# Audio tower on one core: expert up weights loaded tile by tile into a ring of eight instead of kept and copied on chip

## The reference

```python
# _L0_tok_ref: patches of 16 steps, 90 channels -> 192 features
h = einsum('bnf,ef->bne', patches, W) + b                 # 64 clips x 15 tokens, f = 1440
# _L0_attn_ref on layernorm(h): one head of 192 over the 15 tokens of a clip
qkv = einsum('bnd,de->bne', x, W_qkv) + b_qkv
context = einsum('bqk,bkd->bqd', softmax(q k^T / sqrt(192)), v)
h = h + context
# _L0_ffn_ref on layernorm(h): 16 experts, the best 4 of each token
t = rmsnorm(x, norm_scale)
top_vals, top_idx = top_k(t gate_w^T + gate_b, 4);  route_w = softmax(top_vals)
u = einsum('nh,ech->nec', t, mlp1_w) + mlp1_b             # 192 -> 768, per expert
a = swiglu(u)                                             # limit 7, 768 -> 384
y = einsum('nec,ehc->neh', a, mlp2_w) + mlp2_b            # 384 -> 192
h = h + (x + einsum('neh,ne->nh', y, comb))               # comb: the routing weights
```

## Time and profile before

| what | value |
|---|---|
| median of 3 runs | 297.06 us (295.59 to 300.19) |
| the profiled execution | 297.97 us, span 296.1 us |
| TensorE busy | 261.7 us (88%) |
| VectorE, ScalarE, POOL busy | 168.8, 113.4, 174.2 us |
| mean granted TensorE clock | 0.913 |
| DMA | 32.86 MB, mean 111 GB/s |
| from 34 to 68 us | TensorE busy 34.0 us |
| from 200 to 250 us | TensorE busy 50.0 us, DMA share 0.37 |

### The profile page before, as it was taken

How to read it: one execution, slowest core, us unless ns; L and a number is a source line. 1 busy time by engine, 2 the same in 40 slices (tenths; PEclk the granted TensorE clock), 3 DMA queues, 4 the chain that set the end, 5 groups by cost and what they waited for, 6 DMA issues and landing times.

```text
span 296.1 us, 6296 instructions
## 1 busy us (share of the span) xinstructions
PE 261.7 (88%) x1943; PEld 253.7 (86%) x1943; DVE 168.8 (57%) x427; ACT 113.4 (38%) x291; POOL 174.2 (59%) x202
## 2 busy tenths in 40 slices
PE   2869999998757899999999999999999999999800
PEld 1869999998535699999999999999999999999700
DVE  0020246557788647667666666676677666666500
ACT  1001111224307235555455555455555455555200
POOL 5011146668799614667776767766666876663422
PEclk9995999999755579999999999999999999999955
DMA  6999999999999151334333334333333432443211
GB/s 178 231 193 238 242 225 225 269 249 245 266 269 218 43 133 30 57 44 62 53 56 47 60 51 59 56 48 51 58 57 49 66 58 42 56 60 41 26 19 13
DMA packets 18734, 32.86 MB, mean 111 GB/s; under 512 B 3725, under 2 KB 12269, under 8 KB 18701
## 3 DMA queue, kind: packets, MB, share of 16 engines
q1 hardware_dynamic: 6887, 21.60, 30.5%
q0 software_dynamic: 8640, 9.22, 21.4%
q10 hardware_dynamic: 3174, 1.63, 2.4%
HBM read 26.39 MB, written 6.06 MB: 110 GB/s over the span
## 4 chain that ended last, share of the span: by engine, by line
PE 28%; DMA 28%; issue 16%; POOL 11%; POOLq 7%; DVE 5%; SPq 2%; ACT 0%; DVEq 0%
DMA out<-hn_all,put_row 23%; PE bank L908 8%; POOL hn_all L460 7%; POOLq L467 6%; PE bank L1102 5%; DMA qkvw<-in_qkv_w 5%; POOL out L476 4%; PE bank L945 2%; PE bank L937 2%; PE bank L917 1%; PE bank L1051 1%; PE bank L1111 1%; PE bank L954 1%; PE bank L985 1%; DVE x_sb L817 1%
## 5 line engine op out<-in xcount | busy, mean ns | idle before, releaser
L1102 PE MATMUL bank<-xT,x_sb 96*128 96x128 f32 (+1 forms) x1080 | 137.0, 277 | 0.8 <-DVE x_sb L861 0.8
L1102 PEld LDWEIGHTS bank<-xT,x_sb 96*128 96x128 f32 (+1 forms) x1080 | 131.8, 193 | 1.2 <-issue 1.2
L476 POOL DMA_INDIRECT out<-hn_all,put_row x45 | 71.4, 1586 | 56.2 <-DMA out<-hn_all,put_row 24.1
L460 POOL DMA_INDIRECT hn_all<-t_rows,get_row x45 | 50.5, 1121 | 14.7 <-issue 13.4
L1111 PE MATMUL bank<-w_sb,tokw 128*128 x270 | 51.5, 327 | 0.7 <-DVE tokw L883 0.7
L908 PE MATMUL bank<-tokw,x_sb 120*120 120x192 f32 x192 | 38.7, 365 | 6.7 <-DMA x_sb<-in_x 6.7
L1111 PEld LDWEIGHTS bank<-w_sb,tokw 128*128 128x128 f32 x270 | 42.9, 190 | 1.0 <-issue 1.0
L908 PEld LDWEIGHTS bank<-tokw,x_sb 120*120 120x120 f32 x192 | 36.2, 209 | 7.7 <-DMA x_sb<-in_x 7.7
L872 DVE TENSOR_SCALAR ln_all<-bank 128x384 f32<-128x384 f32 x45 | 25.1, 558 | 28.7 <-PE bank L1102 28.7
L876 DVE TENSOR_TENSOR ln_all<-ln_all 128x384 f32<-128x384 f32 x45 | 25.2, 559 | 26.5 <-ACT ln_all L628 26.5
L607 ACT COPY x_sb<-w_sb 96x768 f32 x45 | 37.1, 824 | 6.5 <-PEq L1094 4.2
(11 more groups left out here) (144 smaller groups left out, 237.4 us busy)
## 6 DMA issues: line engine op xcount, KB each, us to landing
w_sb<-in_w SPq DMA_DIRECT2D x16, 576.0 KB, 17.7
x_sb<-in_x SPq DMA_DIRECT2D x7, 675.0 KB, 10.0
w_sb<-in_w SPq DMA_DIRECT2D x16, 288.0 KB, 19.9
t_rows<-hn_all ACTq DMA_DIRECT2D x8, 90.0 KB, 8.5
hn_all<-t_rows,get_row POOLq DMA_INDIRECT x45, 3.2
out<-h ACTq DMA_DIRECT2D x1, 720.0 KB, 5.1
out<-hn_all,put_row POOLq DMA_INDIRECT x45, 3.5
tokw<-in_tok_w SPq DMA_DIRECT2D x1, 540.0 KB, 7.0
```

The costliest lines, as they stand in the source:

```text
L460: g.indirect_dma_start(out=xg[slot], out_offset=None, in_=t_rows, in_offset=bass.IndirectOffsetOnAxis(ap=get_row[:, m:m + 1], axis=0),).th ...
L476: g.indirect_dma_start(out=out, out_offset=bass.IndirectOffsetOnAxis(ap=put_row[:, m:m + 1], axis=0), in_=ysb[m % RING], in_offset=None, c ...
L1102: ins = t.matmul(dst[:, m * SLOTS:(m + 1) * SLOTS], stage[0:rows, j % 2, c, o:o + 128], xT[0:rows, j % 2, c, :], start=(c == 0), stop=(c = ...
```

## The change

The up weights are no longer kept. `w1_sb` becomes a ring of eight buffers. SP reads the owner of each tile and loads that expert's up weights and their bias for the tile, when the tile of eight before has made its second half. TensorE multiplies straight out of the ring. The copies, `stage`, `here` and their semaphores go. Besides: the attention weights are loaded ahead of x of tile 1, the fold stands between the embeddings of tiles 0 and 1, and POOL's first root stands ahead of its wait for the small loads; SP, not ScalarE, stores h, behind two tiles' weights; the down weights come four per tile; the three later bias products stand ahead of the row sums, and their additions ahead of the copy of the rows; the scatter drops rows past the output, so that the extra rows aren't filled, and padding counts as one owner.

```diff
-SETTLED = 12
+WRING = 8
-        w1_sb = sb("w1_sb", [128, E * W1E])
+        w1_sb = sb("w1_sb", [128, WRING * W1E])
...
+        w1_ring = w1_sb[0:HK + 1, :].rearrange("p (b c n) -> p b c n", b=WRING, c=HC)
...
@@ block.sync
-            def load_expert(e):
-                sp.dma_start(w1_sb[0:HK, e * W1E:(e + 1) * W1E], w1[e]).then_inc(s_w[e], 16)
-                sp.dma_start(w2_sb[:, e * W2E:(e + 1) * W2E], w2[e]).then_inc(s_w[e], 16)
+            def load_down(e):
+                sp.dma_start(w2_sb[:, e * W2E:(e + 1) * W2E], w2[e]).then_inc(s_w2, 16)
+
+            sp.dma_start(tokb_sb[:, :], tok_b.broadcast_to([TT, H])).then_inc(s_tokb, 16)
+            sp.dma_start(qkvw_sb[:, :, 0:3 * H + 1], qkv_w).then_inc(s_qkvw, 16)
+            sp.dma_start(qkb_sb[:, :], qk_b).then_inc(s_qkvw, 16)
+            sp.dma_start(vb_sb[:, :], v_b.broadcast_to([TT, H])).then_inc(s_small, 16)
             for i in range(1, TILES):
...
+                if i > RING:
+                    for e in range(4 * (i - RING - 1), 4 * (i - RING)):
+                        load_down(e)
+            sp.wait_ge(s_owner, 1)
+            experts = []
+            for j in range(MT):
+                if j % GROUP == 0:
+                    experts.extend(owners(mybir.EngineType.SP, j // GROUP))
+                if j == 2:
+                    sp.wait_ge(s_b2c, 4)
+                    sp.dma_start(out[0:TOKENS, :].rearrange("(i p) n -> p i n", p=TT), h[:, :, :]).then_inc(s_base_out, 16)
+                if j >= WRING:
+                    sp.wait_ge(s_lin, j - WRING + 1)
+                b = j % WRING
+                sp.dma_start(w1_sb[0:HK, b * W1E:(b + 1) * W1E],
+                             w1[bass.ds(experts[j], 1)].rearrange("a p n -> (a p) n")).then_inc(s_w1[b], 16)
+                sp.dma_start(w1_sb[HK:HK + 1, b * W1E + 2 * I:(b + 1) * W1E],
+                             b1[:, bass.ds(experts[j], 1), :].rearrange("a e n -> (a e) n")).then_inc(s_w1[b], 16)
...
@@ block.gpsimd
-            pool.wait_ge(s_small, 16 * N_SMALL)
             for i in range(AHEAD):
                 root(i)
+                if i == 0:
+                    pool.wait_ge(s_small, 16 * N_SMALL)
                 v_bias(i)
...
                                      in_=ysb[m % RING], in_offset=None, compute_op=ALU.add,
+                                     bounds_check=TOKENS - 1, oob_is_err=False,
...
@@ block.scalar
-            act.wait_ge(s_w[0], 32)
-            act.dma_start(out[TOKENS:TOKENS + SLOTS, :], w2_sb[:, 0:H]).then_inc(s_base_out, 16)
...
-                a.copy(stage[0:HK, j % 2, 0, :], w1_sb[0:HK, bass.ds(experts[j] * W1E, 2 * I)]).then_inc(s_stage_0, 1)
...
-            act.wait_ge(s_b2c, 4)
-            act.dma_start(out[0:TOKENS, :].rearrange("(i p) n -> p i n", p=TT), h[:, :, :]).then_inc(s_base_out, 16)
...
@@ block.vector
             d.tensor_copy(owned[:, :], ps_owner).then_inc(s_owner, 1)
+            dve.wait_ge(s_base, TILES)
+            for q in range(4):
+                dve.wait_ge(s_b2, q + 1)
+                d.tensor_tensor(h[:, 2 * q:2 * q + 2, :], h[:, 2 * q:2 * q + 2, :], ps_b2[q],
+                                ALU.add).then_inc(s_b2c, 1)
             dve.wait_ge(s_rows, 1)
...
-            for back in (1, 2):
-                d.scalar_tensor_tensor(out=landed[:, back - 1, back:MT], in0=owned[:, back:MT],
-                                       scalar=float(E), in1=landed[:, back - 1, back:MT],
-                                       op0=ALU.is_ge, op1=ALU.max).then_inc(s_apart, 1)
...
-                d.tensor_copy(stage[:, j % 2, 1, :],
-                              w1_sb[0:HK + 1, bass.ds(experts[j] * W1E + 2 * I, 2 * I)]).then_inc(s_stage_1, 1)
...
@@ block.tensor
-            for i in range(AHEAD):
-                embed(i)
-            pe.wait_ge(s_small, 16 * N_SMALL)
-            pe.wait_ge(s_qkvw, 16)
+            embed(0)
+            pe.wait_ge(s_qkvw, 32)
             fold_weights()
             pe.wait_ge(s_const, 7)
             turn_h(0)
+            embed(1)
+            pe.wait_ge(s_small, 16 * N_SMALL)
...
             bias2(0)
-
+            bias2(1)
             pe.wait_ge(s_ended, 1)
             t.matmul(ps_owner, ones[0:E, 0:1], ended[:, :], start=True, stop=True).then_inc(s_own, 1)
+            pe.wait_ge(s_pos, 1)
+            for q in range(2, 4):
+                bias2(q)
...
-                        ins = t.matmul(dst[:, m * SLOTS:(m + 1) * SLOTS], stage[0:rows, j % 2, c, o:o + 128],
+                        ins = t.matmul(dst[:, m * SLOTS:(m + 1) * SLOTS], w1_ring[0:rows, j % WRING, c, o:o + 128],
...
-                pe.wait_ge(s_stage_0, j + 1)
-                pe.wait_ge(s_stage_1, j + 1)
+                pe.wait_ge(s_w1[j % WRING], 32 * (j // WRING + 1))
...
+                    if j == 1:
+                        pe.wait_ge(s_w2, 16 * E)
                     down(j - 1)
```

More of the change, by code:

```diff
@@ L212, in audio_tower_kernel @@
         s_qkvw = sem("s_qkvw")
[L213 to L216, removed]
+        s_w1 = [sem(f"s_w1_{b}") for b in range(WRING)]
+        s_w2 = sem("s_w2")
+        N_SMALL = 5
         s_tokb = sem("s_tokb")
@@ L592, in copy_weight @@
             def copy_weight(j):
+                if j % GROUP == 0:
+                    experts.extend(owners(mybir.EngineType.Activation, j // GROUP))
                 if j >= GATHERS:
@@ L596, in copy_weight @@
                 a.copy(weight[:, slot:slot + 1], xg[slot][:, bass.ds(experts[j] + H, 1)]).then_inc(s_weight, 1)
-            def stage_half(j):
-                if j == 0:
-                    act.wait_ge(s_rows, 1)
-                act.wait_ge(s_here, min(j, SETTLED) + 1)
-                if j >= 2:
-                    act.wait_ge(s_lin, j - 1)
-                if j % GROUP == 0:
-                    experts.extend(owners(mybir.EngineType.Activation, j // GROUP))
-                a.copy(stage[0:HK, j % 2, 0, :], w1_sb[0:HK, bass.ds(experts[j] * W1E, 2 * I)]).then_inc(s_stage_0, 1)
             def copy_y(j):
@@ L845, in _ @@
             ins.then_inc(s_table, 1)
-            dve.wait_ge(s_base, TILES)
-            for q in range(4):
-                dve.wait_ge(s_b2, q + 1)
-                d.tensor_tensor(h[:, 2 * q:2 * q + 2, :], h[:, 2 * q:2 * q + 2, :], ps_b2[q],
-                                ALU.add).then_inc(s_b2c, 1)
-            experts = []
-            def stage_half(j):
-                dve.wait_ge(s_here, min(j, SETTLED) + 1)
-                if j >= 2:
-                    dve.wait_ge(s_lin, j - 1)
-                if j % GROUP == 0:
-                    experts.extend(owners(mybir.EngineType.DVE, j // GROUP))
-                d.tensor_copy(stage[:, j % 2, 1, :],
-                              w1_sb[0:HK + 1, bass.ds(experts[j] * W1E + 2 * I, 2 * I)]).then_inc(s_stage_1, 1)
-            stage_half(0)
             for j in range(MT):
-                if j + 1 < MT:
-                    stage_half(j + 1)
                 dve.wait_ge(s_glu, j + 1)
@@ L1069, in _ @@
             ins.then_inc(s_rows, 1)
-            pe.wait_ge(s_pos, 1)
-            for q in range(1, 4):
-                bias2(q)
-            pe.wait_ge(s_b1, 16)
             experts = []
@@ L1085, in turn_x @@
                 ins.then_inc(s_xT, 1)
-            def here(j):
-                if j < SETTLED:
-                    pe.wait_ge(s_ready, pe.value_load(owner[0:1, j:j + 1], min_val=0, max_val=E - 1) + 1)
-                if j == SETTLED:
-                    pe.wait_ge(s_ready, E)
-                if j <= SETTLED:
-                    pe.sem_inc(s_here, 1)
             def up(j, part, dst):
@@ L1115, in _ @@
             pe.wait_ge(s_owner, 1)
-            here(0)
-            here(1)
             pe.wait_ge(s_b2c, 1)
```

28 lines of the change are left out of this document (2 added, 26 removed).

## The result

The changed kernel takes 305.64 us (median of 4 runs, 305.37 to 309.08), the kernel before beside it 298.62 us. The ratio is 1.034, interval 1.021 to 1.047. I had said 297 with a range of 286 to 309 and no measurable change as the likeliest; it became slower by over 2%, to which I had given 0.28. The profiled execution took 305.87 us, its span 303.9 us, against 297.97 and 296.1. All medians in this document are over all executions of a kernel, and all ratios over those that did not fall into the slow state (one of e5 took 449.6 us, at a mean granted clock of 0.565). The kernel before was measured again beside each group of experiments, at 298.5 to 299.5 us.

What follows compares the result with a forecast made beforehand. TensorE's loop, the start, the hand-over and the end were taken as the path, with POOL having no spare time. Terms -6.0 + 3.0 + 10 - 7.1 = -0.1 gave 297.0 against the median, said as 297 us, range 286 to 309.

Steps and rivals of the forecast that it cites:

- the hand-over +3.0 us: Attention to expert loop: bias products ahead of row sums and a first gather beside queued loads cost 3.0 us, between 0 and 4.3.
- the loop's +10: Expert loop: weight transfers make scatters land in 4.8 us on average, POOL falls behind; cost 10 us, bounds 0 and 29.
- Front, -6.0: Start: attention weights land sooner, the fold starts at 15.5 us at full clock; gain 6.0 us, bounds 2.6 and 6.0.
- End, -7.1: After the last copy of y: padding tiles no longer wait for earlier scatters; gain 7.1 us, bounds 5.5 and 8.5.
- The copies, 0: Expert loop: removing the up-weight copies on ScalarE and VectorE gains 0, since TensorE is full.
- The round between queues: DMA engines alternate queues by packet, so a scatter waits behind up to one tile's weights, 2.4 us, landing in 5.9.
- POOL as the bound: Rival, expert loop: a full queue makes scatters land in about 5.6 us, loop cost 23 us, time 310; chance 0.22.
- That the transfers fit: Rival, expert loop: landing stays at or below 4.1 us as loads and scatters alternate or overlap; time 287, chance 0.30.
- The front that does not pay: Rival, start: the clock is lost in the fold, gain 2.6 instead of 6.0 us; time 300, chance 0.10.

Runs made afterwards that it cites:

- e5: e1 plus, from tile 3 on, never more than three weight loads on their way; 307.08 us, ratio 1.028.
- e7: The changed kernel with the store of h behind the first eight loads instead of behind two; 308.17 us, ratio 1.032.
- e1: The changed kernel with the store of h and the loads of tiles 2 to 7 held until the first four gathers landed; 309.54 us, ratio 1.030.
- e2: The changed kernel with only the first eight tiles' up weights loaded, 37 loads left out; 293.56 us, ratio 0.977.
- e9: The changed kernel with only the first half of each tile's up weights loaded from the ninth tile on; 293.72 us, ratio 0.986.
- e6: e5 with eight gather buffers; 300.06 us, ratio 1.002.
- e3: The changed kernel with eight gather buffers instead of four; 303.55 us, ratio 1.014, unclear.
- e4: The kernel before, up weights kept, with the other edits, save that ScalarE still stores h and down weights travel with up weights; 292.92 us, ratio 0.971.
- e8: e4 with the loads of experts 11 to 15 held back until four gathers have landed; 294.67 us, ratio 0.986.
- e10: e8 with the loads of experts 11 to 15 issued one by one at tiles 3, 7, 11, 15 and 18; 289.81 us, ratio 0.971.
- e12: The kernel before with the padding edit alone: padding as one owner, rows past the output dropped; 290.93 us, ratio 0.976.
- e11: The kernel before with the new order of the front alone; 300.05 us, ratio 1.011.

## Why the prediction was wrong

Two steps failed. The sum gave the hand-over +3.0 us with the first gather landing after 3.2 to 5.3 us; it landed after 11.4 us, and the hand-over cost 8.7. And the loop's +10 was worked out from late scatters alone, with the gathers taken as covered; what the loop lost, 11.8 us, began with the gathers. The measured terms are -5.4 for the front, +8.7, +11.8 and -7.3, together the 7.8 us of the spans.

*Front, -6.0.* Right: 5.4 by the embeddings. The fold started at 15.4, and the granted clock read 1.00 where it had read 0.56. That the profiled execution shows the gain is in part luck: in three of the twelve profiles with this order of the front tile 1 came 3 to 4 us later (last section). The fold has twelve one-column records, not the eight that I counted; the sum does not use the number.

*Hand-over, +3.0.* Measured +8.7: the first up product came 3.3 us later while the front came 5.4 sooner. The bias products were to cost 2.4 us and cost 1.3: I took eight groups of row sums at 0.46 us from a row in which the groups stood apart because each waited for its inputs; 32 sums in a row take 2.58 us. The first gather is the step that failed. I had written that seven loads and h queue up, and had a row for a transfer beside a full queue (8.5 us), but used the gather beside one transfer. With that row the sum would have been 101.2 + 8.5 + 1.0 = 110.7 for the up product, 7.5 us late instead of 3.0, and the forecast 301.5. e7 shows that the wait is mostly the weights, e1 that it goes when they are held.

*Loop, +10.* The size came near (11.8), but by luck: the way was another. e2 and e9 show that the bytes cause the loss, as I had said, and e6 shows TensorE waiting through the copy of y as I described. But in the changed kernel what stops TensorE is the gather that stands behind a waiting scatter on POOL and then lands late itself. I had put the scatters' landings at 4.8 us and left the gathers' own out, taking their lead of three tiles as cover, where it is 5.7 us. The steps to a new expert averaged 4.74 us, a landing of 3.8, so by my own formula the loop should have lost nothing. The gathers' two extra microseconds, which I had in the rows and used only as a stand-in for the scatters, made the stops. e3 confirms it: with more gather buffers 7 of the 11.8 us go.

*End, -7.1.* Right: 7.3 in the trace, 7.5 as an experiment of its own.

*The copies, 0.* Right as far as TensorE goes. I had read in the Trainium skill (SBUF — State Buffer, the note on the "DVE blocks DMA" trap) that a VectorE copy from SBUF to SBUF keeps GpSimd from writing descriptors, and priced it at 0.12 us a gather, without counting it. These runs bear out little of it. Gathers took POOL 1.12 us on average before and 1.03 in the changed kernel; but they take 1.04 to 1.06 in e4, e8, e10 and e12, which keep the copies and change the padding, and 1.01 to 1.05 in the kernels without copies. In e11, with copies and the old padding, it is 1.12. So most of the difference goes with the padding edit, and some hundredths of a microsecond a gather at most are left for the copies.

*The round between queues.* The Trainium skill (DMA: Bandwidth & Descriptors, "Queues, rings and completion order") says that each DMA engine goes round between its queues, a packet at a time. From it I took a bound of one tile's weights on a delay, 2.4 us. That bound was mine. It held in the loop, where a gather with about one load on its way was 2 us late, and it broke at the hand-over, where the first gather, with three loads and h issued ahead of it and five loads behind, was 8 us late. The order of packets itself no trace here shows.

*The rivals.* POOL as the bound gave 310 from a scatter's landing of 5.6 us; the time came near it for another reason. That the transfers fit is out, though its condition held on average: by the steps to a new expert the scatters landed in 3.8 us, and the loop lost all the same. The front that does not pay didn't come in the changed kernel's profile, but what it priced, 3.4 us lost in and behind the fold, is about what e3, e10 and e11 show.

Open stays how the DMA engines share among the queues. The runs show that the delay grows with what is queued, not by which order of packets.

## What to carry to other kernels

Before moving resident data to loads in a loop, look at the small transfers on which that loop turns (gathers, scatters, a routing store) and give each the landing time of a full queue, not of an idle one, both at the fill and in the steady state. Then set it against the time between its issue and its use as the trace shows it, not against the number of buffers. A fill can't be paced away when it has to pass the same loop: held loads came back as late scatters in e1 and e8, and only spreading few loads thinly (e10) or halving the bytes (e9) made them nearly free. When several edits are made at once, run each alone: here the padding edit alone was worth the whole gain, and the ring took back more than the others gave.

## What had not been expected of the hardware

The cost of the loads in the loop is a step, not a slope: 0, 0.29 and 0.59 MB per tile gave loops of 178.6, 180.2 and 190.0 us (e2, e9, the changed kernel), with gathers landing in 3.1, 3.6 and 5.0 us. The step is this kernel's, by what the rows show: a cover of 5.7 us hides the first two and not the third once a scatter ahead is late too, and with a cover of 17.9 us (e3) the full load's loop is 183.0.

Rows that POOL's scatter drops cost it no more than written ones: 1.55 us for each of the last scatters in e12, as before.

TensorE ran the front at two speeds with the same granted clock of 1.00. In the changed kernel 39 matmul records began between 20 and 26 us, in e10 26 in the same window, and tile 1 was embedded at 26.09 instead of 22.84. The windows of both:
```profile
20.00:26.00 6.00, 6.00 (x39) 6.00 (x38) 1.47 (x5) 0.00 (x0) 1.33 (x3) 1.00 0.65 160
```
```profile
20.00:26.00 6.00, 6.00 (x26) 6.00 (x26) 0.00 (x0) 0.67 (x5) 0.00 (x0) 1.00 0.96 216
```
In e10 8 records began in each two microseconds up to 24 us and 14 in the next two; in the changed kernel it was 8 from 13 to 15 us and 15 from 20 to 22. So both run at about half pace at first, and differ in when they leave it. The slow front was seen in the profiles of e3 and e11 as well, and not in the other nine with this front. The edits of the front are the same in all, so which comes is not set by them; what sets it, and how often it comes in executions that weren't profiled, these runs don't show.
